# Last layer of a two-layer transformer kernel: its 1024x1024 product in seven block products per pair of token tiles (Strassen's form)

## What is computed

```python
def _L1_ffn_ref(x, W, b, A, B, router_W, router_b):
    q = x[:, 179:-1, :].mean(axis=1)
    routing = softmax(q @ router_W.T + router_b)        # 8 experts, one row per batch
    base = x @ W.T + b                                  # the 1024x1024 product
    t = einsum('bsd,erd->bser', x, A)                   # 8 experts x rank 16 = 128 columns
    lora = einsum('bser,eor,be->bso', t, B, routing) * 2
    return base + lora
# called as
x = x + _L1_attn_ref(_layernorm(x), ...)                # ends with  out @ wo.T
x = x + _L1_ffn_ref(_layernorm(x), ...)
```

## Time and profile before

| | |
|---|---|
| device time, three runs | 1597.60, 1598.59, 1601.69 us; median 1598.59 |
| span of the profiled execution, first to last instruction | 1596.5 us |
| PE busy | 1539.0 us, 96% of the span |
| DVE, ACT, POOL busy | 65%, 55%, 51% |
| output projection, tiles one by one | some 20.7 us a tile, the last one ends at 1372.9 |
| last layer, first matmul to the end of the span | 1374.9 to 1596.5 us |

### The profile page before, as it was taken

The page is one execution under the profiler, slowest core; times in us unless marked ns, Lnnn a source line. Parts: engine busy times, 40 slices in busy tenths (PEclk is TensorE's granted clock), DMA queues, the critical chain, the costliest instruction groups (busy, mean ns, idle before and its releaser), DMA issues. The chain is left out here.

```text
span 1596.5 us, 32012 instructions
## 1 busy us (share of the span) xinstructions
PE 1539.0 (96%) x12384; PEld 948.8 (59%) x12384; DVE 1030.4 (65%) x2745; ACT 878.4 (55%) x1665; POOL 806.3 (51%) x706
## 2 busy tenths in 40 slices
PE   5998999999999999999999999999999999999998
PEld 4656555555556777677777777644444444566564
DVE  8898869986778888888888888742110100444433
ACT  6887324323769999999999999941110000211110
POOL 4223244446948888888888888820100000244450
PEclk9999999999999999999999999999999999999999
DMA  9994245545939999999999999988763330223331
GB/s 366 317 327 149 67 94 145 159 132 127 165 83 165 190 179 180 189 189 198 186 199 186 194 177 188 187 214 221 192 150 79 80 93 1 87 62 80 93 80 66
DMA packets 556503, 248.78 MB, mean 156 GB/s; under 512 B 498368, under 2 KB 531264, under 8 KB 556224
## 3 DMA queue, kind: packets, MB, share of 16 engines
q1 hardware_dynamic: 556352, 246.74, 67.1%
HBM read 73.68 MB, written 48.23 MB: 76 GB/s over the span
## 5 line engine op out<-in xcount | busy, mean ns | idle before, releaser
L2128 POOL TENSOR_TENSOR xb<-xb 128x1280 f16<-128x1280 f32 x128 | 335.7, 2623 | 5.3 <-ACT xb L2031 5.3
L2023 ACT ACTIVATE xb<-bk,D_sv,qw_c 128x512 f32<-128x512 f32 (+3 forms) x512 | 289.1, 622 | 2.4 <-DVE D_sv L2086 2.2
L2077 DVE TENSOR_REDUCE bk<-bk 128x1 f32<-128x512 f32 (+3 forms) x512 | 227.8, 491 | 15.9 <-PE bk L1973 15.2
L2031 ACT ACTIVATE xb<-xb 128x1280 f16<-128x1280 f32 x128 | 162.7, 1271 | 12.2 <-DMA xb<-xb 8.5
L92 POOL TENSOR_SCALAR mv<-mv 128x1 f32<-128x1 f32 x64 | 27.6, 431 | 279.4 <-DVE mv L87 278.3
L1988 PE MATMUL D_t<-vh,xb 128*128 128x65 f16 x1280 | 130.8, 194 | 1.6 <-DVE D_on L2096 1.6
L1989 PE MATMUL D_t<-vl,xb 128*128 128x65 f16 x1280 | 130.9, 192 | 0.0
L1990 PE MATMUL D_t<-vh,xb 128*128 128x65 f16 x1280 | 130.3, 193 | 0.0
L2246 DVE SCALAR_TENSOR_TENSOR xb<-bk,ms_c,xb 128x512 f32<-128x512 f32 x22 | 15.5, 746 | 166.0 <-PE bk L50 166.0
L1988 PEld LDWEIGHTS D_t<-vh,xb 128*128 128x128 f16 x1280 | 118.7, 97 | 2.5 <-issue 2.2
L1989 PEld LDWEIGHTS D_t<-vl,xb 128*128 128x128 f16 x1280 | 118.4, 98 | 0.4
(11 more groups left out here) (367 smaller groups left out, 4627.5 us busy)
## 6 DMA issues: line engine op xcount, KB each, us to landing
od<-D_os SPq DMA_DIRECT2D x32, 512.0 KB, 4.6
xd<-xb SPq DMA_DIRECT2D x16, 512.0 KB, 4.0
ow_raw<-mwd SPq DMA_DIRECT2D x32, 256.0 KB, 3.4
xb<-xd SPq DMA_DIRECT2D x16, 512.0 KB, 5.9
out_x<-xb SPq DMA_DIRECT2D x16, 512.0 KB, 2.9
xb<-in_x SPq DMA_DIRECT2D x6, 1024.0 KB, 14.3
A_wo<-in_wo SPq DMA_DIRECT2D x6, 1024.0 KB, 6.8
ow_raw<-in_w SPq DMA_DIRECT2D x16, 384.0 KB, 4.6
```

The costliest lines, as they stand in the source:

```text
L2023: m = e.activation(p[:, AT[i]:AT[i] + N], Sb[n % 4][:, c:c + N], ACT.Exp, scale=qw.col(qw.NEG, g), bias=s[:, 7 - i:8 - i])
L2031: e.activation(P2[u % 3][:, 0:1280], P[u % 3][:, :], ACT.Copy).then_inc(s_ph, 1)
L2077: m = e.tensor_reduce(minima(u, i), Sb[n % 4][:, c:c + N], AX.X, ALU.min)
L2128: e.tensor_tensor(P2[u % 3][:, 1280:2560], P[u % 3][:, :], P2[u % 3][:, 0:1280], ALU.subtract).then_inc(s_pl, 1)
```

## The change

The 1024x1024 product of two token tiles is done in Strassen's form (with Winograd's sums). Let a pair of tiles be the upper and lower rows and split the features in two halves, and W into four blocks of 512x512. Eight block products become seven. They need three differences of the operands made ahead, on the activation side `sa` and `sb` (each two halves long) and on the weight side four sums `T1` to `T4`. Each product is 4 slices x 3 matmuls of 512 columns.

- **Weights** (`LastWeights`, in the output projection). They are loaded and squared in 11 pieces (two DMAs each). From tile 6 (`TOTALS`) on, eight items of 4 x 256 columns are loaded again. POOL makes four sums of each, ACT the high halves, DVE the low halves, both of the three remaining source quarters and of the sums, into one buffer `O`, from which SP stores them to DRAM (`w1d`). Three smaller items follow (the 136 router and A columns twice, which stay in SBUF, and B, which is stored too). DVE makes the low halves after it has added tiles 7, 8 and 9 (`LOWS`). The seven blocks, 1 MB each, are loaded back: one in step 11, three during the last tile, into memory whose projection weights are used up, and three in the last layer.
- **Activations** (`PairFeed`). Four operands are normalized or summed, split and turned for each pair of tiles, where there were two. The pair's tiles are t and t+2.
- **Last layer.** `gates` makes the 136 columns of a pair in matmuls of their own. Then come seven products, each cut in halves, with the small steps between halves. Products add to the same bank where the form wants a sum, and DVE reads the bank after each product and adds it to where `GOES` says.
- **Semaphores.** Those of `first` are cleared by POOL early in `lora_layer0` and used again.

```diff
 def out_projection(...)
-    NORMED, TOTALS = 3, 9
+    TOTALS = 6
+    LOWS = {7: (0, 1, 2), 8: (3, 4, 5), 9: (6, 7, 8, 9, 10)}
...
     def act(e):
-        for n in range(lw.N):
-            lw.act_square(e, w, n)
...
-        for n in range(4):
-            lw.act_split(e, w, n)
+        for v in range(4):
+            pf.act_high(e, w, v)
+            if v == 1:
+                for q in range(lx.N):
+                    lx.act_square(e, w, q)
+        for n in range(len(lx.ITEMS)):
+            lx.act_high(e, w, n)
...
     def dve(e):
         for j in range(NT):
             add(j)
...
+            for n in LOWS.get(j, ()):
+                lx.dve_low(e, w, n)
...
     def sp(e):
         for j in range(G, NT):
             w.wait_ge(s_col, j - 2)
             ow.sp_turn(e, j)
...
+            if j == 7:
+                pf.sp_turn(e, w, 2)
+                for n in range(3):
+                    lx.sp_load(e, w, n)
+                w.wait_ge(pf.s_lo, 4)
+            if j == 11:
+                lx.all_stored(w)
+                lx.sp_load_block(e, w, 0)
...
+            for n in LOWS.get(j - 1, ()):
+                if n < 8 or n == 10:
+                    lx.sp_store(e, w, n)
+                if n + 3 < len(lx.ITEMS):
+                    lx.sp_load(e, w, n + 3)
+        for i in range(1, 4):
+            w.wait_ge(lx.s_free, i)
+            lx.sp_load_block(e, w, i)
```

```diff
+class LastWeights:
+    def pool_sums(self, e, w, n):
+        r, t = self.quarters(n), self.T[n % 2]
+        b11, b21, b22, b12 = [r[:, i, :] for i in range(4)]
+        self.landed(w, n)
+        w.wait_ge(self.s_lo, n - 1)
+        e.tensor_tensor(t[:, 0, :], b12, b11, ALU.subtract).then_inc(self.s_sums, 1)
...
+    def act_high(self, e, w, n):
+        w.wait_ge(self.s_sc, 1)
+        self.landed(w, n)
+        if n < 8:
+            w.wait_ge(self.s_sums, 4 * n + 4)
+        w.wait_ge(self.s_out, self.stored_before(n))      # 32 * min(n, 8)
...
+    def dve_low(self, e, w, n):
+        w.wait_ge(self.s_sc, 1)
+        w.wait_ge(self.s_hi, n + 1)
+        for o, src, kind in self.splits(n):               # 128x768 and 128x1024
+            i = e.scalar_tensor_tensor(o[1], src, self.scale(kind), o[0], ALU.mult, ALU.subtract)
+        i.then_inc(self.s_lo, 1)
+    def sp_store(self, e, w, n):
+        x, c = self.ITEMS[n]
+        w.wait_ge(self.s_lo, n + 1)
+        for l in range(2):                                # w1d: [7, 128, 2, 4, 512] float16
+            to, of = self.w1d[:, :, l, x, 256 * c:256 * c + 256].rearrange("b p n -> p b n"), self.O[:, l, :, :]
+            e.dma_start(to, of).then_inc(self.s_out, 16)
```

```diff
 def lora_layer1(...)
+    PRODUCTS = [("X", 0, 0, lx.B11), ("Z", 0, 4, lx.B21), ("X", 2, 4, lx.T2), ("Y", 3, 0, lx.T3), ("X", 2, 0, lx.T1),
+                ("Y", 1, 4, lx.T4), ("X", 3, 4, lx.B22)]
+    GOES = [(0, 0), (0, 0), (1, 0), (1, 1), (1, 1), (1, 0), (0, 1)]
+    EVEN = {11: "r"}
+    ODD = {0: "w0", 2: "a0", 3: "w1", 5: "a1", 6: "w2", 8: "a2", 9: "w3", 11: "a3"}
...
+        gates(0)
+        for p in range(NP):
+            for s in range(14):
+                half_product(p, s // 2, s % 2)
+                x = inside(p, s)
+                if x:
+                    {"r": router, "w": turn_w, "a": adapter}[x[0]](x[1])
+                if s == 9 and p + 1 < NP:
+                    gates(p + 1)
...
     def dve(e):
+        for p in range(NP):
+            fin, adapted = 7 * p, 0
+            if p + 1 < NP:
+                for q in (2 * p + 2, 2 * p + 3):
+                    pf.dve_apply(e, w, q, xb)
+            for s in range(14):
+                if s % 2:
+                    read(p, s // 2, adapted)
...
+                if p + 1 < NP and s in (1, 3):
+                    pf.dve_sums(e, w, p + 1, s // 2)
+                if p + 2 < NP and s == 7:
+                    pf.dve_stats(e, w, 2 * p + 4, xb)
+                    pf.dve_stats(e, w, 2 * p + 5, xb)
...
     def sp(e):
+        e.dma_start(bias[:, :], lx.b1.partition_broadcast(128)).then_inc(lx.s_bias, 16)
+        pf.sp_turn(e, w, 3)
+        for i in range(4, 7):
+            lx.sp_load_block(e, w, i)
...
+        for p in range(NP):
+            if p + 1 < NP:
+                w.wait_ge(s_p, 7 * p)
+                for v in range(4 * p + 4, 4 * p + 8):
+                    pf.sp_turn(e, w, v)
```

More of the change, by code:

```diff
@@ L294, in layers @@
             mid.close()
[L295 to L298, removed]
+            lx.place(lambda name, shape, dt=F: last.enter_context(nc.sbuf_tensor(f"F1_{name}", shape, dt)), ow, xb)
+            pf.place(lambda name, shape, dt=F: last.enter_context(nc.sbuf_tensor(f"P_{name}", shape, dt)), keep, xb)
             out_projection(**g)
@@ L2426, in pe, with gates @@
-        for x in ORDER:
-            if x[0] == "c":
-                columns(x[1], x[2])
-            else:
-                small(x)
+        def gates(p):
+            for i in range(2):
+                hi, lo = pf.halves(4 * p + i)
+                pf.turned(w, 4 * p + i)
+                w.wait_ge(s_ta, 2 * p)
+                for k in range(KD):
+                    x = mm3(e, gb[:, GN * i:GN * i + GN], (hi[:, k, :], lo[:, k, :]), (lx.G[0][:, k, :], lx.G[1][:, k, :]),
+                            k == 0, k == KD - 1)
+                x.then_inc(s_g, 1)
@@ new lines, in half_product @@
+        def half_product(p, i, h):
+            _, kind, k0, blk = PRODUCTS[i]
+            hi, lo = pf.halves(4 * p + kind)
+            W = lx.pe_block(w, blk)
+            pf.turned(w, 4 * p + kind)
+            w.wait_ge(s_fin, read_before(p, i))
+            for k in range(2 * h, 2 * h + 2):
+                x = mm3(e, bank(p, i)[:, :], (hi[:, k0 + k, :], lo[:, k0 + k, :]), (W[0][:, k, :], W[1][:, k, :]),
+                        k == 0 and i in (0, 1, 3), k == 3, skip_group_check=i in (2, 4, 5, 6))
+            if h:
+                x.then_inc(s_p, 1)
@@ L2536, in dve @@
[L2536 to L2558 removed]
+                n = turn_no["a", q, c]
@@ new lines, in adapter, with read @@
+                dst = xb[:, pf.tile(q), 512 * c:512 * c + 512]
+                w.wait_ge(s_tp, n + 1)
+                e.scalar_tensor_tensor(dst, tr[n % 2][:, :], lx.adapters(), dst, ALU.mult, ALU.add).then_inc(s_tr, 1)
+        def read(p, i, adapted):
+            q, c = GOES[i]
+            q += 2 * p
+            dst = xb[:, pf.tile(q), 512 * c:512 * c + 512]
+            w.wait_ge(s_xb, q + 1)
+            w.wait_ge(s_p, 7 * p + i + 1)
+            if i in (1, 4, 5):
+                w.wait_ge(s_fin, 7 * p + {1: 1, 4: 4, 5: 3}[i])
+            w.wait_ge(s_tr, adapted)
+            e.scalar_tensor_tensor(dst, bank(p, i)[:, :], lx.inverse("w"), dst, ALU.mult, ALU.add).then_inc(s_fin, 1)
@@ L2592, in sp, with store @@
-        for t in range(2, NT):
-            if t + 2 < NT:
-                feed.sp_turn(e, w, N1 + t + 2)
-            for c in range(3):
-                for y in inner(t, c):
-                    if y[0] == "a":
-                        store(y[1])
-        for t in (12, 14, 15):
-            store(t)
-        w.wait_ge(s_out, 16 * NT)
+        def store(q, halves=(0, 1)):
+            t = pf.tile(q)
+            for c in halves:
+                e.dma_start(out[128 * t:128 * t + 128, 512 * c:512 * c + 512], xb[:, t, 512 * c:512 * c + 512]).then_inc(s_out, 16)
```

629 lines of the change are left out of this document (373 added, 256 removed).

## The result

The changed kernel takes 1616.01 us (median of 4 runs, 1612.87 to 1619.15), the kernel before 1598.09 (4 runs, 1595.74 to 1601.69): a ratio of 1.011, 95% interval 1.0091 to 1.013. It is 1.1% slower. The forecast was 1607 us, 0.5% slower, with 1600 to 1618 as the range of the case of held turns.

The account below looks back on a forecast made before the run. PE, busy 96% of the span, was taken to bound the kernel. 1596.5 + 26.3 (projection) - 18.3 (last layer) = 1604.5 us of span, plus 2.1 to the runs' median: 1607 us; 8 in 10 for 1588 to 1632.

Parts of the forecast that it names:

- the case of held turns: Projection: SP's turns wait behind stores that wait for DVE's low halves; 1607 us, 1600 to 1618, chance 0.54.
- The terms of the projection: Projection: 24.8 us of delay from turns held on SP plus 1.5 us of slower clock, +26.3 us.
- X: Projection: time for an item's two 448 KB stores to land, taken as 5.0 us, with 3.6 to 9 open.
- the cycle: Projection: one item's stores, ACT's high half, DVE's low half and hand-overs, X + 4.5, so 9.5 us.
- (b): Projection: short stores, X near 3.6, net faster at 1591 us; chance 0.20.
- (c): Projection: slow stores, X at 8, chain 24 us longer, 1631 us; chance 0.17.
- The pauses: Projection: PE idle before tiles 9, 10 and 11 for 11, 8 and 6 us, waiting for turns.
- The last pause's clock: Projection: slower PE clock after the last pause, the only one counted, 1.5 us (0 to 3).
- The saving of the product: Last layer: seven products instead of eight, and adapters inside pair 7, save 23.8 us of PE work and waits.
- rival (e): Last layer: each gate matmul takes a weight load's time, 15 us more, 1622 us; chance 0.04.
- What the last layer pays: Last layer: 3 us at the start plus 2.5 us for adapters' adds behind DVE's statistics, 5.5 us; net gain 18.3 us.
- The start of the last layer: Last layer: pair 1's turns queue behind 4.75 MB of SP's loads and come late to `gates`, 3 us (0 to 5).

Follow-up runs that it names:

- e2_spread: Changed kernel with each projection step's stores issued after the tile's turn and low halves spread over tiles 7 to 10: 1589.21 us, ratio 0.9936 to the kernel before.
- e3_third_store: Changed kernel with a third store of 448 KB for each item, to a tensor nobody reads: 1634.78 us (one run).
- e6_mean_later: e2_spread with activation sums on POOL, and mean matrix and adapter weights loaded behind two turns of pair 1: 1580.39 us, ratio 0.9885 to the kernel before.
- e8_pool_sums_alone: Changed kernel, projection as it was, with only the last layer's activation sums made by POOL instead of DVE: 1610.9 us (one run).
- e7_loads_behind: Changed kernel with stores after each step's turn, and block 0 and four x loads behind tile 12's turn: 1594.99 us, ratio 0.9979 to the kernel before.
- e9_other_form: e2_spread with the activation sums still on DVE, each made by scalar_tensor_tensor instead of tensor_tensor: 1589.35 us (one run).

## Why the prediction was right, and where it was off

**The sign and its cause** held. The time came out at 1616.01 us where 1607 was forecast, and both terms missed to the same side: the projection cost 2.3 us more than I had put, the last layer kept 7.1 us less. SP holds the turns of tiles 9, 10 and 11 behind stores that wait for DVE's low half. Taking the stores out of the way (e2_spread) takes all three pauses away, and adding store (e3_third_store) makes them longer.

**The terms of the projection.** X was put at 5.0 and is 5.16 us; the cycle at 9.5 and is 9.4. That rules out rivals (b) and (c). The nearness of X is in part luck, as the rows left 3.6 to 9 open. The Trainium skill's fit ("DMA: Bandwidth & Descriptors", "Anatomy of one DMA"), for another issuing path, gave an estimate of 4.1 us for the pair of stores; the trace has 5.16 until the engine that waits for them starts. The pauses were put at 11, 8 and 6 us and are 13.15, 4.10 and 3.30. The last turn was due at 1294.2, and tile 11 starts at 1296.3. The second and third pause are shorter because PE comes to them late. From tile 9's first matmul until PE has no work, 1269.71 - 4.10 - 1242.18 = 23.4 us pass where 96 steps of 0.2156 are 20.7. The granted clock in the two stretches shown is 0.74 and 0.81, with matmuls at half speed (the level of 1.2 GHz) right after each pause. I had said that only the last pause's clock counts, as the chain doesn't depend on PE. In one link it does: DVE makes items 6 and on only after it has added tile 9, at 1265.65, late by the first pause, so the stores of items 5 and 6 are issued at 1259.01 and 1269.20, 10.2 us apart. The last pause's clock I put at 1.5 us; from 1296.32 to 1402.48 are 106.2 us for 479 steps, 103.3 at full speed, so it cost 2.9. Measured from tile 7's add, the projection's term is 28.6 us against 26.3: the clock 1.4, the chain on SP 0.9.

**The saving of the product** (23.8 us) held in what it rests on. Gates step by 0.06 us, so rival (e) is out. With e6_mean_later's last layer of 202.1 us (1374.56 to 1576.7), 19.5 us of the 23.8 are there, and its waits of 2.9 at the gates and 1.5 at F_tr are as large as the missing 4.3.

**What the last layer pays** is the step that was mis-sized: 5.5 us were put, and 23.8 - 11.2 = 12.6 were paid. The failing words are "DVE ... stays below 120. Both fit." I costed DVE's and POOL's loads each by itself and never asked whether DVE's new sums could run beside POOL's instructions, of which the same change made more. It put 23 us of waiting into DVE (42.7 - 19.3). PE saw 5.6 us of it in the changed kernel (210.4 - 204.8, e8_pool_sums_alone), so 5.6 of the missing 7.1 are this. I gave F_tr 2.5 us; it lost 5.5, and 1.5 with the sums gone. The other 1.5 is the start of the layer. With the sums gone PE waits 4.0 us at the gates, the clock is 0.72 in the 6 us behind it (1.7 us lost), and F_tr has 1.5: 7.2 where I had put 3 + 2.5. I had charged a slower clock to the projection alone. In the changed kernel itself it is 0.84 from 1414.6 to 1424.6 (1.6 us). This and the 9.2 us of waits are 10.8 of the 12.6 us; the other 1.8 stand in no row shown here.

With a last layer that keeps only 11.2 us, the sign no longer turns at an X of 4.4 us. By my estimate the change would be slower down to an X of 3.0 (28.6 - 8 x 2.2 = 11.0).

**The start of the last layer.** I said 3 us at `gates` of pair 1; the changed kernel shows 0.2. The step was right and hidden: PE had lost 2.79 us in F_X just ahead, which gave the turn its time. With that gone the wait is 4.0 us. The reason was only half right: I counted the bias as bytes ahead of the turn. In the changed kernel the chain that ended last goes from the bias's load (1404.59) to POOL's bias adds (1408.96), its low halves and the turn (1416.19), so the turn waits for compute that waits for that load. No run here loads the bias earlier.

**Semaphores.** POOL still waits 9.32 us for DVE there, and goes on at 149.32 where the earlier trace rows has 149.37: free, as said.

**What stays open.** The clock's share after a pause is read from rows and not tried by itself. It was 2.9 us after the last pause of the changed kernel (3.30 us long) and 1.6 after the single one of e7_loads_behind (4.62 us; 384 matmuls from 1295.13 to 1379.33). The rows of the 6 us behind each pause have the difference, granted 0.53 and 0.74:

```profile
1296.30:1302.30 6.00, 5.98 (x15) 2.14 (x16) 0.00 (x0) 0.00 (x0) 0.00 (x0) 0.53 1.00 352
```

```profile
1295.10:1301.10 6.00, 5.97 (x21) 2.44 (x22) 0.00 (x0) 0.00 (x0) 0.00 (x0) 0.74 0.99 341
```

Why the clock stayed low for longer after the shorter pause, and why it fell after 2.79 us in the changed kernel and not after 2.50 in e9_other_form, no run here says.

## What to carry to other kernels

Read a change for what it puts ahead of a load on the queue that issues it, stores that wait for compute above all, and count the loads too: the same work and bytes, in another order, were 27 us apart here (changed kernel and e2_spread). Before new element-wise work goes to VectorE because it has room, look whether it reads two operands from SBUF while GpSimd is busy in the same stretch; if so give it to GpSimd, or expect each instruction to end only after the one that GpSimd has running. Count the slower clock behind each pause wherever it falls. When one wait hides another, the sum of single gains is too high: after each repair read the waits again.

## What the runs showed of the hardware

- A DVE sum of 512 columns with two SBUF inputs takes 0.69 us with POOL idle. Started while a tensor_tensor of POOL runs, it ends 0.55 us after POOL's, and takes up to 2.61; with 2 columns 0.15, and up to 1.50. It holds for tensor_tensor and scalar_tensor_tensor alike. POOL's two low halves beside such sums took 5.11 us, without them 4.21. DVE's reads of a PSUM bank with one SBUF operand keep 0.75 us.
- After pauses of 3.3 to 14.0 us in the projection TensorE ran at half speed for some us, which cost 1.5 to 2.9 us more each. In the last layer the same came after 2.79 us (0.84 in 10 us), and did not after two of 1.5 and 1.4 us (e6_mean_later, 1.00).
- Two stores of 448 KB from SBUF to DRAM in rows of 512 bytes took 5.16 us from issue to the waiting engine's start (4.96 to 5.98 in eight such waits), a third one about 1.8 us more.
